# Gated cross-attention and a routed feed-forward: experts chosen in three batches, scatters begun inside attention, gathers issued pair by pair

## The chip, the cores and the metric

The kernel runs on one core of a Trainium2 chip. The metric is the device time of one execution in microseconds. "Span" is the time from the first to the last instruction of a profiled execution.

## The reference

```python
x = x + tanh(g_xattn) * attention(layernorm(x), ctx, ctx)       # x: 8 x 256 x 256, ctx: 8 x 77 x 256, 16 heads
n = layernorm(x)                                                # the kernel's x2
logits = n @ gate_w.T                                           # 8 experts
top_w, sel = top_k(softmax(logits), 2); top_w /= sum(top_w)
y = sum over the 2 chosen e of  w_e * (gelu(n @ W1[e] + b1[e]) @ W2[e] + b2[e])    # 256 -> 1024 -> 256
x = x + tanh(g_ffn) * (y + gelu(n @ sW1 + sb1) @ sW2 + sb2)     # + the shared expert, for every row
```

Everything is float32.

## The kernel before

The 2048 rows are `NT` = 16 tiles of 128. The kernel has two stages.

**Attention**, a software pipeline of steps `t` = 0 to 19. A step of PE holds the scores of tile t+1, the transposes and the weighted values of tile t, the projection of t-1, the transposes of the second layer norm's rows (`turn_x2`) of t-3 and the router's logits of t-4 (`route_logits`). DVE subtracts the maxima, normalises (L1242), adds the residual (`residual`, which waits on `x2_ready` of the tile ahead) and keeps the logits. ACT exponentiates and copies PSUM. POOL makes `x2row` (L461, `normal_two(t - 2)`), the layer-normed row tile; SP copies it into `x2` (`keep_x2`). POOL also loads the shared expert's weights in quarters and splits them into a high and a low part (`split_quarter_1`, `split_quarter_2`), in steps 5 to 12. Step 15 ends with `up(0)`, the first matmuls of the next stage.

**Expert stage**, `TILES` = 55 tiles of 128 rows: first `NA` = 9 "early" tiles through the shared expert, then `NR` = 39 "routed" tiles, grouped by expert, each expert's group padded to whole tiles, then `NB` = 7 "late" tiles through the shared expert. `R0` = 9 is the first routed tile and `R1` = 48 the first late one. For tile i PE runs `turn_hidden(i-1)` (L729, 8 transposes), `up(i)` (L741 to L743, 12 matmuls in two halves), `turn_rows(i+1)` (L722), `down(i-1)` (L754, L755, 16 matmuls). ACT copies the transposed hidden rows (L1111) and runs Gelu (L1117). DVE forms their low parts (L1271), adds b1 (L1277), forms the rows' low part (`rows_lo`, L1265) and makes the result (`ysum` L1387, `yrow` L1394, and for tiles of the shared expert L1400). SP loads each tile's rows two tiles ahead (`load_rows`), ACT stores a routed result to `routed_y` in HBM.

**Routing** stands between. After the last logits DVE picks the two experts of all 16 tiles (L1368 to L1383; `then` makes each operation wait for the one before). PE counts places with 17 small matmuls (`places`, in tile 1). `slots` (DVE, tile 1) turns counts into a destination row for each of the 4096 pairs of row and expert. `tables` and `tile_phases` (tiles 2 and 3) say which expert each tile has. POOL then issues 32 indirect DMAs (L619, the scatters: tile by tile, one for each of the two choices, 128 rows of 1 KB), which copy `x2` into `routed_x` in HBM. SP waits for all of them (`scattered`) before the first routed load. `routed_x` is zeroed by SP beforehand, in 6 parts after the `keep_x2` of steps of late attention (L363), since the padding rows must hold numbers.

After the last routed result is stored, POOL issues 32 indirect gathers (L655), and DVE adds them to the output in the late tiles (`combine`, L1416, two operations for each of the 16 tiles; `COMBINED` says in which late tile). `g_in[j]` counts the four gathers of output tiles 2j and 2j+1.

POOL also streams the experts' weights during the routed tiles (`phase`). Its queue is in order. Before the scatters it holds two quarters of `load_quarter_2` (L485, L486), four `split_quarter_1` (L491), four `split_quarter_2` (L497) and two loads of 1 MB.

## Time and profile before

| | us |
|---|---|
| median of three runs | 647.6 |
| lowest and highest of them | 638.16, 649.21 |
| the profiled execution | 643.06 |
| its span | 641.5 |
| PE busy | 551.5 (86%) |
| DVE, POOL, ACT busy | 357.8, 292.1, 242.0 |
| PE's mean granted clock | 0.91 of full |

Busy shares are means over stages that have different limits. The page's line of 40 slices shows where an engine is idle, the timeline shows which instruction ends an idle stretch, and the bracket behind a row gives how long its engine had been idle and what released it. "remote" in a bracket is a semaphore whose raising the trace can't place at that time.

### The profile page before, as it was taken

Reading aid. Unit: us, or ns where it says so; the run is one execution under the profiler, and the core shown is the slowest. Engines: PE = TensorE matmul, PEld = TensorE weight load, DVE = VectorE, ACT = ScalarE, POOL = GpSimd, SP = SyncE. Lnnn points to the kernel's source line nnn. Section 1 sums busy time; section 2 is a strip of 40 time slices with the busy share of each in tenths; the row PEclk is TensorE's granted clock in tenths of the full one; section 3 lists DMA queues with packets and bytes.
Section 4 is the critical chain, followed back from the end, with each engine's and each line's share of the span. In section 5 each row is a group of like instructions: output and inputs, shape, how many; then the busy total and the mean of one; then the engine's idle time right before and its main releaser. Section 6 shows DMA issues by size and latency. Waiting matters only on the chain.

```text
span 641.5 us, 12348 instructions
## 1 busy us (share of the span) xinstructions
PE 551.5 (86%) x3243; PEld 478.4 (75%) x3244; DVE 357.8 (56%) x735; ACT 242.0 (38%) x534; POOL 292.1 (46%) x267
## 2 busy tenths in 40 slices
PE   4799899998976841999999999999999999951496
PEld 3699899998965620888888888888888888840385
DVE  4346776655639510757556565565655655520398
ACT  3123576665641200333433334333333343310132
POOL 6226478885437774004354444444545430077300
PEclk9957799989886955899999999999999999995699
DMA  4752556567846332006556678486666640143211
GB/s 131 198 167 79 157 145 172 171 188 229 255 159 203 106 107 74 16 26 216 148 200 179 206 207 237 122 245 214 185 203 180 204 114 33 41 114 105 84 50 65
DMA packets 62216, 95.21 MB, mean 148 GB/s; under 512 B 6653, under 2 KB 47853, under 8 KB 62197
## 3 DMA queue, kind: packets, MB, share of 16 engines
q0 software_dynamic: 24800, 57.82, 30.7%
q1 hardware_dynamic: 28885, 29.77, 14.5%
q10 hardware_dynamic: 8512, 7.40, 3.8%
q8 instruction: 9, 0.15, 0.1%
q14 instruction: 10, 0.08, 0.0%
HBM read 68.15 MB, written 20.71 MB: 139 GB/s over the span
## 4 chain that ended last, share of the span: by engine, by line
PE 69%; DVE 9%; issue 8%; another core or an unknown queue 7%; ACT 3%; DMA 3%; ACTq 1%; POOL 0%; DVEq 0%; SPq 0%; POOLq 0%
PE ps L754 15%; PE ps L755 7%; PE ps L741 7%; PE ps L742 7%; PE ps L743 7%; PE ps L729 7%; PE ps L812 3%; PE ps L768 3%; PE ps L707 3%; PE ps L798 2%; PE ps L780 2%; PE ps L722 2%; DVE rt L1375 1%; DMA front<-in_ctx 1%
## 5 line engine op out<-in xcount | busy, mean ns | idle before, releaser
L754 PE MATMUL ps<-w2hl,hTh 128*128 (+1 forms) x440 | 164.6, 411 | 14.0 <-DVE hTl L1271 12.7
L1117 ACT ACTIVATE hid<-hid 128x512 f32<-128x512 f32 x110 | 69.2, 632 | 161.3 <-DVE hid L1277 150.3
L755 PE MATMUL ps<-w2hl,hTl 128*128 (+1 forms) x440 | 124.9, 284 | 0.0
L1111 ACT ACTIVATE hTh<-ps 128x512 fp32r<-128x512 f32 x110 | 60.1, 597 | 132.4 <-PE ps L729 87.6
L754 PEld LDWEIGHTS ps<-w2hl,hTh 128*128 128x128 f32 x440 | 84.2, 191 | 34.2 <-issue 16.9
L1277 DVE TENSOR_TENSOR hid<-ps,b1bc 128x512 f32<-128x512 f32 x110 | 75.3, 690 | 53.9 <-PE ps L743 22.4
L741 PE MATMUL ps<-w1l,xT 128*128 (+1 forms) x220 | 94.4, 429 | 11.1 <-issue 6.6
L742 PE MATMUL ps<-w1h,xT 128*128 (+1 forms) x220 | 89.1, 405 | 3.9 <-issue 3.9
L743 PE MATMUL ps<-w1h,xT 128*128 (+1 forms) x220 | 89.0, 404 | 3.0 <-issue 3.0
L755 PEld LDWEIGHTS ps<-w2hl,hTl 128*128 128x128 f32 x440 | 84.5, 192 | 0.0
L729 PE MATMUL ps<-ident,hid 128*128 128x128 f32 x440 | 60.2, 281 | 24.8 <-ACT hid L1117 18.9
L1271 DVE TENSOR_TENSOR hTl<-ps,hTh 128x512 fp32r<-128x512 f32 x110 | 71.0, 685 | 6.0 <-issue 6.0
L729 PEld LDWEIGHTS ps<-ident,hid 128*128 128x128 f32 x440 | 51.9, 145 | 29.0 <-ACT hid L1117 20.2
L1387 DVE TENSOR_TENSOR ysum<-ps,b2bc 128x256 f32<-128x256 f32 x55 | 23.3, 424 | 78.6 <-PE ps L755 45.0
L514 POOL TENSOR_TENSOR w2hl<-stage,w2hl 128x2048 f32 (+1 forms) x8 | 36.9, 4613 | 54.9 <-DMA w2hl<-in_L_ffn_W 49.8
L741 PEld LDWEIGHTS ps<-w1l,xT 128*128 128x128 f32 x220 | 42.9, 195 | 20.9 <-issue 8.7
L506 POOL TENSOR_TENSOR w1l<-stage,w1h 128x2048 f32 (+1 forms) x8 | 36.9, 4616 | 41.9 <-DMA w1h<-in_L_ffn_W 35.8
L743 PEld LDWEIGHTS ps<-w1h,xT 128*128 128x128 f32 x220 | 42.6, 194 | 13.5 <-issue 3.0
L742 PEld LDWEIGHTS ps<-w1h,xT 128*128 128x128 f32 x220 | 43.1, 196 | 11.1 <-issue 3.4
L1265 DVE TENSOR_TENSOR xT<-ps,xT 128x256 fp32r<-128x256 f32 x55 | 23.3, 424 | 50.0 <-ACT xT L1021 44.8
L655 POOL DMA_INDIRECT gath<-routed_y,slot x32 | 30.5, 952 | 44.2 <-DMA routed_y<-yrow 34.8
L812 PEld LDWEIGHTS ps<-spread_v,probT 128*128 128x128 f32 (+1 forms) x320 | 41.4, 199 | 1.2
(178 smaller groups left out, 846.2 us busy)
## 6 DMA issues: line engine op xcount, KB each, us to landing
stage<-in_L_ffn_W POOLq DMA_DIRECT2D x14, 1024.0 KB, 6.1
w1h<-in_L_ffn_W POOLq DMA_DIRECT2D x7, 1024.0 KB, 5.9
w2hl<-in_L_ffn_W POOLq DMA_DIRECT2D x7, 1024.0 KB, 8.4
qstack<-moved_q SPq DMA_DIRECT2D x48, 128.0 KB, 2.4
xrow<-routed_x SPq DMA_DIRECT2D x39, 128.0 KB
routed_y<-yrow ACTq DMA_DIRECT2D x39, 128.0 KB, 2.3
routed_x<-zeros SPq DMA_DIRECT2D x6, 768.0 KB, 5.8
moved_q<-hid SPq DMA_DIRECT2D x16, 256.0 KB, 3.6
```

The costliest lines, as they stand in the source:

```text
L506: pool.tensor_tensor(lo, stage1[:], hi.bitcast(F32), ALU.subtract).then_inc(S["split_w1"], 1)
L729: last = nc.tensor.transpose(p_hT[:, n, c, :], hid[:, n, c * P:(c + 1) * P], ident[:])
L741: mm(p_h[:, n, :], xTh[:, c, :], part(w1l, c), start=c == 0, stop=False)
L742: mm(p_h[:, n, :], xTh[:, c, :], part(w1h, c), start=False, stop=False)
L743: last = mm(p_h[:, n, :], xTl[:, c, :], part(w1h, c), start=False, stop=c == C - 1)
L754: mm(p_y, hTh[:, c, :], part(2 * D), start=c == 0, stop=False)
L755: last = mm(p_y[:, 0:D], hTl[:, c, :], part(D), start=False, stop=c == FC - 1)
L812: last = mm(p_o[:, h0:h1, :], probT[0:n, j, :], spread_v[0:n, at:at + h1 - h0, bass.ds(t // TB, 1), :].rearrange("k n o d -> k (n o) d"), ...
L1111: act.activation(hTh[:, n * (FC // 2):(n + 1) * (FC // 2), :], p_hT[:, n, :, :], ACT.Copy).then_inc(S["hT_hi"], 1)
L1117: act.activation(hid[:, n, :], hid[:, n, :], ACT.Gelu).then_inc(S["h_act"], 1)
L1271: tt(hTl[:, part, :], p_hT[:, n, :, :], hTh[:, part, :].bitcast(F32), ALU.subtract).then_inc(S["hT_lo"], 1)
L1277: tt(hid[:, n, :], p_h[:, n, :], b1bc[:, bass.ds(s, 1), n * (F // 2):(n + 1) * (F // 2)].rearrange("p o f -> p (o f)"), ALU.add).then_inc( ...
```

## The change

The experts are chosen in three batches of tiles, 0 to 7, 8 to 11 and 12 to 15. `choose(0)` runs at the end of DVE's attention step 11 and `choose(1)` at the end of step 15, each followed one step later by PE's `places(n)` and DVE's `slots(n)`; PE waits for `slots_set` at the start of the step after that. `choose(2)` stands where the one choice stood. `run` carries the counts from batch to batch.

A destination row no longer depends on all counts: `routed_x` has room for 17 tiles per expert (`CAP`), and each pair goes to expert * `CAP` plus its place. Only 8 tiles of padding are zeroed (`pad_row`), after `counts`. SP reads the row at which a routed tile begins from `src_row` with a `value_load`. The gathers use a second table, `y_slot`, since `routed_y` stays packed.

POOL issues twelve scatters of batch 0 by threes in its steps 13 to 16, with one quarter of `load_quarter_2` and one `split_quarter_1` each; then the other four, `load_w1` and `ready_1`, the 8 of batch 1 and the 8 of batch 2; then the four `split_quarter_2` and `load_w2`.

`NA` becomes 5, so `NB` becomes 11: 5 early, 39 routed, 11 late tiles, `R0` = 5, `R1` = 44. In the gathers POOL waits, before the four of a pair of output tiles, for the landing of the four before. `COMBINED` has eleven entries with at most two tiles each. Some tiles of SBUF are ordered anew, and the counts' PSUM lies in banks 5 and 7.

```diff
-    NA = NT // 2 + 1
+    NA = 5
...
+    CAP = (NT + 1) * P
+    BATCHES = ((0, 8), (8, 12), (12, NT))
+    CHOSEN_AFTER = (11, 15)
...
                 if kind == "routed":
-                    src = rows_v[bass.ds(i - R0, 1)].rearrange("o p d -> (o p) d")
+                    at = sp.value_load(src_row[0:1, bass.ds(i, 1)], min_val=0, max_val=E * CAP - P)
+                    src = rows[bass.ds(at, P), :]
...
-                part = rows_v[n * SHARE:min((n + 1) * SHARE, NR)]
-                sp.dma_start(part.rearrange("t p d -> p t d"), zeros[:].unsqueeze(1).to_broadcast(
-                    [P, part.shape[0], D])).then_inc(S["rows_zeroed"], 16)
-            in_pairs(sp, 2, R0, lambda i, parity: load_rows(i, parity, "early"))
+            load_rows(2, 0, "early")
+            load_rows(3, 1, "early")
+            sp.wait_ge(S["zero_set"], 1)
+            sp.wait_ge(S["pads_set"], 1)
+            for e in range(E):
+                at = sp.value_load(pad_row[0:1, e:e + 1], min_val=0, max_val=E * CAP - P)
+                sp.dma_start(rows[bass.ds(at, P), :], zeros[:]).then_inc(S["rows_zeroed"], 16)
+            in_pairs(sp, 4, R0, lambda i, parity: load_rows(i, parity, "early"))
+            sp.wait_ge(S["src_set"], 1)
+            sp.wait_ge(S["rows_zeroed"], 16 * E)
             sp.wait_ge(S["scattered"], 16 * TOP * NT)
...
-                if 13 <= t < 15:
+                if t == 12:
+                    pool.wait_ge(S["kd_ready"], 2 * B)
+                    pool.iota(tile_i[:], pattern=[[1, TILES], [0, PH - 1]], base=0, channel_multiplier=0
+                              ).then_inc(S["tiles_set"], 1)
+                if 13 <= t < 17:
                     load_quarter_2(1, first_w2, t - 13)
+                    split_quarter_1(1, t - 13)
+                    for n in range(3):
+                        scatter(0, 3 * (t - 13) + n)
+
+            def scatter(batch, n):
+                t, k = BATCHES[batch][0] + n // TOP, n % TOP
+                pool.wait_ge(S["slots_set"], batch + 1)
+                pool.wait_ge(S["x2_out"], 16 * (t + 1))
+                pool.indirect_dma_start(
+                    out=rows, out_offset=bass.IndirectOffsetOnAxis(ap=slot[:, k, t:t + 1], axis=0),
+                    in_=x2[:, t, :], in_offset=None).then_inc(S["scattered"], 16)
 
             for t in range(NT + 2):
                 step(t)
-            load_quarter_2(1, first_w2, 2)
-            load_quarter_2(1, first_w2, 3)
-            for q in range(4):
-                split_quarter_1(1, q)
+            for n in range(12, 16):
+                scatter(0, n)
             pool.wait_ge(S["split_w1"], 8)
             load_w1(2, expert_w1(1))
             ready_1(1)
+            for batch in (1, 2):
+                for n in range(TOP * (BATCHES[batch][1] - BATCHES[batch][0])):
+                    scatter(batch, n)
             for q in range(4):
                 split_quarter_2(1, q)
             pool.wait_ge(S["split_w2"], 8)
             load_w2(2, expert_w2(1))
             ready_2(1)
...
-            pool.wait_ge(S["slots_set"], 1)
-            pool.wait_ge(S["rows_zeroed"], 16 * NB)
-            pool.wait_ge(S["x2_out"], 16 * NT)
-            for t in range(NT):
-                for k in range(TOP):
-                    pool.indirect_dma_start(
-                        out=rows, out_offset=bass.IndirectOffsetOnAxis(ap=slot[:, k, t:t + 1], axis=0),
-                        in_=x2[:, t, :], in_offset=None).then_inc(S["scattered"], 16)
...
+            pool.wait_ge(S["y_slots_set"], 1)
             for t in range(NT):
+                if t % 2 == 0 and t:
+                    pool.wait_ge(g_in[t // 2 - 1], 16 * 2 * TOP)
                 for k in range(TOP):
                     pool.indirect_dma_start(
                         out=gath[:, t, k, :], out_offset=None, in_=routed_y,
-                        in_offset=bass.IndirectOffsetOnAxis(ap=slot[:, k, t:t + 1], axis=0)
+                        in_offset=bass.IndirectOffsetOnAxis(ap=y_slot[:, k, t:t + 1], axis=0)
                     ).then_inc(g_in[t // 2], 16)
...
+            def places(n):
+                t0, t1 = BATCHES[n]
+                wide, p_place = t1 - t0, p_places[n]
+                pe.wait_ge(S["chosen_set"], n + 1)
+                if n == 0:
+                    pe.wait_ge(S["q_sb"], NT)
+                if n == 1:
+                    pe.wait_ge(S["x2T_sb"], CHOSEN_AFTER[1] - 1)
+                mm(p_place[:, 0:wide + 1, :], before[:], chosen[:, t0 + n:t1 + n + 1, :], start=True, stop=False)
+                for u in range(wide):
+                    last = mm(p_place[:, u + 1:wide + 1, :], ones[:],
+                              chosen[:, t0 + n + u:t0 + n + u + 1, :].to_broadcast([P, wide - u, E]),
+                              start=False, stop=u == wide - 1)
+                last.then_inc(S["rank_ps"], 1)
...
+                if known and t - 2 in CHOSEN_AFTER:
+                    pe.wait_ge(S["slots_set"], CHOSEN_AFTER.index(t - 2) + 1)
...
+                if known and t - 1 in CHOSEN_AFTER:
+                    places(CHOSEN_AFTER.index(t - 1))
...
+            def choose(n):
+                t0, t1 = BATCHES[n]
+                some = [P, t1 - t0, E]
+                bc = lambda ap: ap.unsqueeze(2).to_broadcast(some)
+                far = iota_far[:].unsqueeze(1).to_broadcast(some)
+                if n == 0:
+                    dve.wait_ge(S["kd_ready"], 2 * B)
+                    dve.wait_ge(S["far_set"], 1)
+                    dve.memset(chosen[:], 0.0)
+                    dve.memset(run[:], 0.0)
+                dve.wait_ge(S["l_sb"], t1)
+                for k in range(TOP):
+                    lg = (logits, lg2)[k][:, t0:t1, :]
+                    then(dve.tensor_reduce(top[:, k, t0:t1], lg, AX_X, ALU.max))
+                    then(tt(rt[:, t0:t1, :], lg, bc(top[:, k, t0:t1]), ALU.is_equal))
+                    then(tt(rt[:, t0:t1, :], rt[:, t0:t1, :], far, ALU.mult))
+                    then(dve.tensor_reduce(pick[:, k, t0:t1], rt[:, t0:t1, :], AX_X, ALU.min))
+                    then(tt(hot[:, k, t0:t1, :], far, bc(pick[:, k, t0:t1]), ALU.is_equal))
+                    if k == 0:
+                        then(stt(lg2[:, t0:t1, :], hot[:, 0, t0:t1, :], -1e30, logits[:, t0:t1, :], ALU.mult, ALU.add))
+                tt(chosen[:, t0 + n:t1 + n, :], hot[:, 0, t0:t1, :], hot[:, 1, t0:t1, :], ALU.add
+                   ).then_inc(S["chosen_set"], 1)
+
+            def slots(n):
+                t0, t1 = BATCHES[n]
+                wide, p_place = t1 - t0, p_places[n]
+                dve.wait_ge(S["rank_ps"], n + 1)
+                then(tt(place[:, t0:t1, :], p_place[:, 0:wide, :], run[:].unsqueeze(1).to_broadcast([P, wide, E]), ALU.add))
+                then(tt(run[:], run[:], p_place[:, wide, :], ALU.add))
+                then(tt(onplace[:, :, t0:t1, :], hot[:, :, t0:t1, :],
+                        place[:, t0:t1, :].unsqueeze(1).to_broadcast([P, TOP, wide, E]), ALU.mult))
+                then(dve.tensor_reduce(posf[:, :, t0:t1], onplace[:, :, t0:t1, :], AX_X, ALU.add))
+                then(stt(slot_f[:, :, t0:t1], pick[:, :, t0:t1], float(CAP), posf[:, :, t0:t1], ALU.mult, ALU.add))
+                ts(slot[:, :, t0:t1], slot_f[:, :, t0:t1], FAR * CAP, None, ALU.add).then_inc(S["slots_set"], 1)
...
+                if isinstance(t, int) and t - 1 in CHOSEN_AFTER:
+                    slots(CHOSEN_AFTER.index(t - 1))
+                if isinstance(t, int) and t in CHOSEN_AFTER:
+                    choose(CHOSEN_AFTER.index(t))
...
+            choose(2)
+            rows_lo(1)
...
-            COMBINED = ((), (0, 1), (2, 3, 4), (5, 6, 7), (8, 9, 10), (11, 12), (13, 14, 15))
+            COMBINED = ((), (), (0, 1), (2, 3), (4, 5), (6, 7), (8, 9), (), (10, 11), (12, 13), (14, 15))
...
+            def counts():
+                slots(2)
...
+                then(stt(pad_f[:], iota_far[0:1, :], float(CAP), run[0:1, :], ALU.mult, ALU.add))
+                ts(pad_row[:], pad_f[:], FAR * CAP, None, ALU.add).then_inc(S["pads_set"], 1)
...
+            def sources():
+                then(dve.memset(step_up[:], 0.0))
+                then(ts(step_up[0:1, 1:E], etiles[0:1, 0:E - 1], -float(P), float(CAP), ALU.mult, ALU.add))
+                then(ts(limit[:], etiles[0:1, E - 1:E], float(P), float((E - 1) * CAP - P), ALU.mult, ALU.add))
+                then(tt(ups[:], started[0:1, :, 0:E], step_up[:].unsqueeze(1).to_broadcast([1, TILES, E]), ALU.mult))
+                then(dve.tensor_reduce(src_f[:, 0, :], ups[:], AX_X, ALU.add))
+                then(stt(src_f[:, 1, :], tile_f[0:1, :, 0], float(P), src_f[:, 0, :], ALU.mult, ALU.add))
+                then(ts(src_f[:, 0, :], src_f[:, 1, :], -float(R0 * P), None, ALU.add))
+                tt(src_row[:], src_f[:, 0, :], limit[:].to_broadcast([1, TILES]), ALU.min).then_inc(S["src_set"], 1)
...
+            def y_slots():
+                then(tt(onplace[:], hot[:], ebase[:].unsqueeze(1).unsqueeze(1).to_broadcast([P, TOP, NT, E]), ALU.mult))
+                then(dve.tensor_reduce(slot_f[:], onplace[:], AX_X, ALU.add))
+                stt(y_slot[:], slot_f[:], float(P), posf[:], ALU.mult, ALU.add).then_inc(S["y_slots_set"], 1)
...
+            def late_tables():
+                shares()
+                y_slots()
+
+            tile(1, "early", 0, 0, between=counts)
             tile(2, "early", 0, 0, between=tables)
-            tile(3, "early", 0, 0, between=tile_phases)
-            tile(4, "early", 0, 0, between=shares)
-            dve.wait_ge(S["tables_set"], 2)
+            tile(3, "early", 0, 0, between=sources)
+            tile(4, "early", 0, 0, between=late_tables)
```

## Rows read from the trace of the kernel before

**Rows 1.** The page's 40 slices of 16 us, PE's busy tenths

```profile
PE   4799899998976841999999999999999999951496
```

**Rows 2.** Table of stretches: stretch, its us, busy us of each engine, PE clock, DMA share, GB/s

```profile
300.00:500.00 200.00, 200.00 (x1137) 171.93 (x1135) 117.08 (x210) 78.49 (x151) 87.89 (x51) 1.00 0.65 196
...
560.00:610.00 50.00, 20.95 (x87) 15.30 (x85) 11.70 (x23) 6.24 (x13) 30.40 (x32) 0.68 0.34 97
```

**Rows 3.** Timeline of DVE, `ysum`: start us, us, engine, line, operation, idle before

```profile
217.56 0.42 DVE L1387 TENSOR_TENSOR ysum<-ps,b2bc 128x256 f32<-128x256 f32 x1 [2.42 <-remote]
...
255.28 0.42 DVE L1387 TENSOR_TENSOR ysum<-ps,b2bc 128x256 f32<-128x256 f32 x1 [20.31 <-remote]
...
563.31 0.42 DVE L1387 TENSOR_TENSOR ysum<-ps,b2bc 128x256 f32<-128x256 f32 x1 [0.95 <-issue]
...
605.60 0.42 DVE L1387 TENSOR_TENSOR ysum<-ps,b2bc 128x256 f32<-128x256 f32 x1 [9.80 <-remote]
...
612.78 0.42 DVE L1387 TENSOR_TENSOR ysum<-ps,b2bc 128x256 f32<-128x256 f32 x1 [0.31 <-PE ps L755]
...
620.13 0.42 DVE L1387 TENSOR_TENSOR ysum<-ps,b2bc 128x256 f32<-128x256 f32 x1
...
626.92 0.42 DVE L1387 TENSOR_TENSOR ysum<-ps,b2bc 128x256 f32<-128x256 f32 x1
```

**Rows 4.** Timeline of POOL: first and last of 32 scatters and of 32 gathers

```profile
209.52 1.09 POOL L619 DMA_INDIRECT routed_x<-x,slot  x1 [4.67 <-DVE slot L1453]
...
249.39 0.97 POOL L619 DMA_INDIRECT routed_x<-x,slot  x1 [0.30 <-issue]
...
559.94 1.02 POOL L655 DMA_INDIRECT gath<-routed_y,slot  x1 [34.80 <-DMA routed_y<-yrow]
...
598.90 0.95 POOL L655 DMA_INDIRECT gath<-routed_y,slot  x1 [0.30 <-issue]
```

**Rows 5.** Timelines of PE, ACT and DVE: PE's signals and who takes them

```profile
215.65 1.03 PE L729 MATMUL ps<-ident,hid 128*128 128x128 f32 x8
...
219.08 0.40 PE L743 MATMUL ps<-w1h,xT 128*128 128x512 f32 x1
...
219.68 0.60 ACT L1111 ACTIVATE hTh<-ps 128x512 fp32r<-128x512 f32 x1 [5.25 <-remote]
...
232.48 0.69 DVE L1277 TENSOR_TENSOR hid<-ps,b1bc 128x512 f32<-128x512 f32 x1 [6.35 <-remote]
...
563.11 1.03 PE L729 MATMUL ps<-ident,hid 128*128 128x128 f32 x8
...
568.68 0.60 ACT L1111 ACTIVATE hTh<-ps 128x512 fp32r<-128x512 f32 x1 [2.30 <-remote]
```

**Rows 6.** Table of stretches, behind the last scatter

```profile
251.50:252.00 0.50, 0.00 (x0) 0.00 (x0) 0.00 (x0) 0.00 (x0) 0.00 (x0) 0.50 0.00 0
```

**Rows 7.** Timeline of POOL: a split, and `x2row` in late attention steps

```profile
100.19 1.29 POOL L491 TENSOR_TENSOR w1l<-stage,w1h 128x512 fp32r<-128x512 f32 x1
...
170.44 0.77 POOL L485 DMA_DIRECT2D stage<-in_L_ffn_W  x1
...
175.07 1.21 POOL L461 TENSOR_SCALAR x2row<-xres,mv,nw 128x256 f32<-128x256 f32 x1 [3.14 <-ACT nw L1044]
...
187.65 1.22 POOL L461 TENSOR_SCALAR x2row<-xres,mv,nw 128x256 f32<-128x256 f32 x1 [5.13 <-ACT nw L1044]
```

**Rows 8.** Timeline of DVE: two operations of the choice of experts

```profile
197.97 5.02 DVE L1375 TENSOR_TENSOR rt<-lg,top 128x128 f32<-128x128 f32 x1
...
203.03 0.29 DVE L1376 TENSOR_TENSOR rt<-rt,iota_far 128x128 f32<-128x128 f32 x1
```

**Rows 9.** Timeline of DVE: one normalisation per attention step

```profile
149.80 0.42 DVE L1242 TENSOR_TENSOR o_n<-ps,rsum 128x256 f32<-128x256 f32 x1
...
157.71 0.42 DVE L1242 TENSOR_TENSOR o_n<-ps,rsum 128x256 f32<-128x256 f32 x1
...
167.60 0.42 DVE L1242 TENSOR_TENSOR o_n<-ps,rsum 128x256 f32<-128x256 f32 x1
```

More of the change, by code:

```diff
@@ L923, in _ @@
                 step(t, t % 2)
-            def places():
-                pe.wait_ge(S["chosen_set"], 1)
-                mm(p_place, before[:], chosen[:], start=True, stop=False)
-                for u in range(NT):
-                    last = mm(p_place[:, u + 1:NT + 1, :], ones[:],
-                              chosen[:, u:u + 1, :].to_broadcast([P, NT - u, E]), start=False, stop=u == NT - 1)
-                last.then_inc(S["rank_ps"], 1)
             def phase_at(i):
@@ L954, in _ @@
             turn_rows(1, 1)
-            tile(1, 1, (0, 0), (0, 0), places)
+            tile(1, 1, (0, 0), (0, 0), lambda: places(2))
             in_pairs(pe, 2, R0, lambda i, parity: tile(i, parity, (0, 0), (0, 0)))
@@ L1436, in tile @@
                 result(i - 1, phase_at(i - 1) if last is None else last, kind)
-            def slots():
-                dve.wait_ge(S["rank_ps"], 1)
-                then(ts(cnt_i[:, 0, :], p_place[:, NT, :], float(P - 1), None, ALU.add))
+            def counts():
+                slots(2)
+                then(ts(cnt_i[:, 0, :], run[:], float(P - 1), None, ALU.add))
                 then(ts(cnt_i[:, 1, :], cnt_i[:, 0, :], 7, None, ALU.logical_shift_right))
```

74 lines of the change are left out of this document (28 added, 46 removed).

## The prediction

> **What bounds the kernel now.** I read the page first: in [rows 1] TensorE is full in nearly all 40 slices of 16 us, but two stretches are almost empty, slices 15 to 16 (225 to 257 us) and slices 36 to 38 (560 to 610 us). The table of stretches [rows 2] shows them against a full one: from 300 to 500 us PE is busy for all 200 us at full clock, from 560 to 610 us for 20.95 of 50.
>
> Next the list of `ysum`, one per tile of the expert stage. From tile 2 (255.28) to tile 48 (563.31) there are 46 tiles in 308.03 us [rows 3]: 6.70 us a tile, with PE never idle. So PE sets the pace, and the change leaves PE's work on the 55 tiles alone. What it can move are the two gaps: tile 1 to tile 2 took 37.7 us, 31.0 more than 6.7 (the first gap); tile 48 to tile 49 took 42.3, 35.6 more (the second gap) [rows 3]. The time after is that of now less what of these 66.6 us comes back, plus what the new work costs.
>
> Then what runs beside each gap. POOL issues its 32 scatters from 209.52 to 250.36 and its 32 gathers from 559.94 to 599.85 without a pause, one each 1.27 us [rows 4]. Nobody waits for their data in either gap. What comes late is PE's word to the others [rows 5]. The transposes of one tile begin at 215.65, and ACT, which starts 0.6 us into them in a quiet tile, starts at 219.68; the last matmul of `up` begins at 219.08, and DVE's add of its second half is at 232.48, 13 us late. In the gather series the second half of the transposes begun at 563.11 reaches ACT at 568.68, 4.5 us late. So PE's signals are prompt for some 3.4 us, late by 2 to 5 us at an age of 4 to 7 us, and after about 15 us everybody stands. It ends at 255.28, 4.9 us after the last scatter, and at 605.60, 5.7 us after the last gather, although the DMA engines moved nothing after 251.5 [rows 6]. I take the cause as "a long unbroken series of indirect DMAs holds up PE's signals". I don't know the path on which they meet.
>
> **The change, part by part, against the profiled execution** (643.1 us, of which the span is 641.5; the three runs have their median at 647.6 and their lowest at 638.2, so the one stands between them and I take the sum as the forecast of the median).
>
> *A, attention: +5.* Sixteen scatters of batch 0 become ready at step 12; twelve are issued by threes in POOL's steps 13 to 16, with the four `split_quarter_1` (1.29 us each [rows 7]). POOL's step 14 then holds 1.2 of `x2row`, 1.5 of two loads (0.77 each), 1.3 of split and 3.8 of scatters, 7.8 us, and the steps there are 6.3 us apart (175.07 to 187.65 in two) [rows 7]. POOL's slack is used up in step 14, `x2row` is then late by 2, 3.5 and 5 us, and the last one (187.65) carries the last logits: +5 (0 if the steps stretch anyway, 8 at most). DVE's `residual` queues behind `x2_ready`, and PE's next scores behind DVE; I count that in the same 5. `choose` is 13 operations; uncontended, they lie 0.32 us apart [rows 8], 4.2 us for each early batch on DVE. DVE is half idle in these steps, so 1 us is charged for two. `slots(0)` isn't hidden: PE has just run `places(0)` (9 small matmuls, at 0.13 us like the transposes of [rows 5] or twice that: 1 to 2 us) and stops at the next step for six DVE operations, 1.9 us; the second batch lies in steps that wait for the `x2row` chain. Together +4 with the other batch's matmuls. To the credit: SP's zeroing of 5 MB (39 tiles of 128 KB) beside these steps is gone; eight writes of 128 KB remain, behind the early loads. The step that ends at 167.60 took 9.9 us, its forerunner 7.9 [rows 9], and nothing shows that it was the zeroing: I credit 3 (0 to 5). The last batch's `choose(2)` handles 4 tiles and not 16. In the trace one of these two-input operations took 5.03 us beside POOL's four splits, where 0.30 is normal [rows 8]. POOL scatters there after the change. I credit 2, less than half of that stall, since `rows_lo(1)`, for which PE waits, stands ahead of it in DVE's queue. Sum 5+1+4-3-2 = +5, bounds -3 and +15.
>
> The row of 5.03 us is weighed against the Trainium skill, "SBUF — State Buffer", on the shared port pair: an operation of VectorE with both inputs in SBUF and a GpSimd operation that reads SBUF block each other, the later for the whole of the earlier. By that rule the stalls move with the splits: `choose(1)` in step 15 runs beside a split of 1.29 us and would pay up to that much. By the row's whole price (5.03) A would be 9, by the rule at most 6.3.
>
> *B, the first gap: 31 becomes 16.* After step 17 POOL issues 4 and 8 scatters in one series (12 x 1.27 = 15.3 us), stops for `slots_set` of the last batch, and issues 8 more (10.2 us). The first series loses what it outlasts the prompt time: 15.3, plus 2 to 5 us to clear, less the 7 to 9 for which work goes on: 10. DVE's `slots(2)` itself waits for PE's `rank_ps` through this, so the 8 can't join the 12. They lose 10.2 plus 3 less 7: 6. Bounds: 5 (both short series are borne as the first 8 us of the long one were) and 31. Behind the waiting POOL stand `split_quarter_2`, `load_w2` and `ready_2(1)`; they end near 235 us, and `down` of tile 5 wants them near 255: covered by 20 us, and without that cover their 6 us would show. The routed rows wait for the scatters' landing near 230, behind tiles 2 to 4 (3 x 6.7 us): covered.
>
> *C, longer DVE chains in early tiles 1 to 4: +2.* `counts` has 13 operations for 9, `sources` 8 more, `tables` takes over three. DVE is busy 117.08 of 200 us [rows 2], so it has 2.8 us to spare in a tile of 6.7; each chain goes over that by about 0.5 (0 and 6 as bounds). SP's extra `value_load` before each routed load costs nothing: the load is two tiles ahead (13 us); without that cover it costs its own latency, once.
>
> *D, the second gap: 35.6 and 1.1 of slow clock behind it become 6.* Four gathers take 3 x 1.25 us to the last issue, which lands after some 2.1 us (the last scatter was issued at 249.39 [rows 4], and nothing moved after 251.5 [rows 6]). With 0.7 for the wait's own latency a pair has 6.6 us, the eight 53 us. They start 3.4 us before the first late tile's `ysum`, like now, and eleven late tiles give 74 us: pair n is wanted about 13 + 6.7n us after that `ysum` and a step later from pair 5 on, so the combining waits for nothing; at a period of 10 us it would wait some 15 at the end. What remains is lateness inside a burst of 4.7 us: signals late by 2 to 4.5 us, where PE's order (`turn_hidden`, then `up` from 216.7 to 219.5, then `down`) bears about 2, which is these 2.8 less ACT's 0.6 [rows 5]. That is 0 to 2 a burst; I take 0.75, so 6. Clearing in the pause is my assumption: 32 in a row needed 4.9 us to clear, 0.15 each, so 4 need 0.6, and the pause is 1.9.
>
> *E, -1.* Combining three outputs stretched a late tile to 7.35 us, two leave it at 6.79 [rows 3], and the last tile now combines two for three.
>
> Sum: 5 - 15 + 2 - 30.7 - 1 = -39.7, and 643.1 - 39.7 gives **603 us**, 0.93 of the median. Its own range is 590 to 620.
>
> **Rivals.**
> *Standstill doesn't clear in a pause (slower).* If the 4.9 us behind a series are fixed, whatever its length, then a pause of 1.9 us between pairs clears nothing, and neither do the 4 us between the threes in attention. For it: both long series show nearly the same tail (4.9 and 5.7). Against it: the lateness grows through the series, as a backlog does. Price: the paced gathers stand for 53 + 5.5 - 8 = 50 us, 14 over now; four attention steps lose 3.8 + 4.9 - 3.4 = 5.3 each, 21; the two series of B lose 13 and 12. 643.1 + 5 + 21 - 6 + 14 + 2 - 1 = 678. It decides as soon as clearing takes more than 1.9 us behind four.
> *A paced burst costs its lateness in full.* Each of the eight costs the 4.5 us of the second half's signal: 36 instead of 6, 633 us. The change then would not do what it says: the gap is only spread out. The rows at 568.68 speak for it, PE's 2 us of slack against it.
> *Short series are free.* B falls to 5 and D to 0: 603 - 11 - 6 = 586. For it are the 3.4 prompt us and 6 us of nearly normal work in the gather series.
>
> The Trainium skill, "Runtime: NRT & Kernel Launch", on instruction fetch, offers another reading of the first rival: instructions stream in pages through a DMA queue, and fetch suffers where execution leaves the window. That would hit the unrolled attention steps and late tiles, of which the change adds; its time would be that rival's. No row here shows such a fetch. Since PE itself ran on (219.08) while DVE had its signal 13 us late [rows 5], I give that reading no chance of its own.
>
> **Chances.** Forecast 0.48, short series free 0.13, lateness in full 0.20, no clearing 0.19. A run under about 635 counts as faster, over 660 as slower (2% is about what this kernel's spread lets one tell). The third case lies across 635; a quarter of it is faster. Faster 0.48 + 0.13 + 0.05 = 0.66, same 0.15, slower 0.19. The range from 584 to 648 leaves out the last case and a little below.
>
> **What the profile after would show.** D right: gathers by fours over 50 to 56 us, PE busy in nine tenths there, late tiles at 6.7 to 8 us. B right: tile 2's `ysum` near 245 and two stretches of idle PE with a run of tiles between. A right: last logits near 196. The rival of no clearing: PE at a few tenths through all eleven late tiles, and attention steps 13 to 16 over 10 us. Lateness in full: late tiles at 10 to 11 us. The forecast would be wrong above all if pauses of 2 us do nothing, or if twelve scatters inside attention hold its chain more than they occupy POOL.

## The result, and the profile after

| | before | after |
|---|---|---|
| median of the runs | 648.4 us (638.16 to 653.22) | 600.03 us (596.85 to 600.65) |
| profiled execution, its span | 643.1 us, 641.5 us | 599.54 us, 597.9 us |
| last logits (end of attention) | 191.28 | 204.61 |
| `ysum` of tile 2 | 255.28 | 247.40 |
| `ysum` of tile 44 (the first late one after) | 536.69 | 527.36 |
| `ysum` of tile 54 (the last) | 637.94 | 594.33 |

The ratio is 0.932, with an interval of 0.919 to 0.945. The ratio leaves out executions in the slower state that a kernel is sometimes in, at a lower granted clock, so it isn't the quotient of the medians: they differ by 48.4 us, the executions that the ratio compares by 43.5. The spans of the two profiled executions differ by 43.6 us. From this table: attention ends 13.3 us later; from there to tile 2 it is 42.8 us where it was 64.0 (-21.2); tiles 2 to 44 take 279.96 where they took 281.41 (-1.4); tiles 44 to 54 take 66.97 where they took 101.25 (-34.3).

The page's slices of the kernel after, 15 us each; `PEclk` is the granted clock in tenths:

```profile
PE   4799899999788573999999999999999999999996
PEclk9765999999879585999999999999999999999999
```

Against [rows 1] the second hole has gone: from slice 17 to the end PE is full. The first has shrunk to slices 14 to 16, and slices 11 and 12, in attention, have thinned to 7 and 8.

Table of stretches of the kernel after, columns as in [rows 2]:

```profile
151.80:164.10 12.30, 8.25 (x60) 7.37 (x59) 10.00 (x26) 5.55 (x17) 4.54 (x6) 0.86 0.52 157
164.10:175.70 11.60, 9.59 (x56) 9.39 (x57) 6.26 (x16) 4.91 (x14) 7.07 (x7) 0.71 0.40 126
204.00:230.00 26.00, 15.72 (x70) 12.30 (x70) 8.15 (x33) 4.99 (x10) 20.50 (x22) 0.70 0.48 165
...
524.00:578.00 54.00, 53.46 (x301) 45.26 (x300) 40.73 (x81) 19.43 (x39) 30.52 (x32) 1.00 0.40 118
```

The last row answers to 560 to 610 in [rows 2]: the same 32 gathers occupy POOL for the same 30.5 us, but PE is busy for 53.46 of 54 us, and at full clock (1.00, that is 2.4 GHz) where it had 0.68. The third row is the first hole: PE works 15.72 of 26 us.

Timeline of DVE after, `ysum`, to be held against [rows 3]:

```profile
231.05 0.42 DVE L1447 TENSOR_TENSOR ysum<-ps,b2bc 128x256 f32<-128x256 f32 x1 [13.87 <-remote]
...
247.40 0.40 DVE L1447 TENSOR_TENSOR ysum<-ps,b2bc 128x256 f32<-128x256 f32 x1
...
527.36 0.42 DVE L1447 TENSOR_TENSOR ysum<-ps,b2bc 128x256 f32<-128x256 f32 x1 [0.92 <-issue]
534.61 0.42 DVE L1447 TENSOR_TENSOR ysum<-ps,b2bc 128x256 f32<-128x256 f32 x1 [0.22 <-issue]
542.61 0.42 DVE L1447 TENSOR_TENSOR ysum<-ps,b2bc 128x256 f32<-128x256 f32 x1 [0.59 <-issue]
...
594.33 0.42 DVE L1447 TENSOR_TENSOR ysum<-ps,b2bc 128x256 f32<-128x256 f32 x1 [0.81 <-PE ps L780]
```

There is now one standstill, 13.87 us long, ahead of tile 0. The ten steps from 527.36 to 594.33 are 6.70 us in the mean (from 5.25 to 8.14), against 6.67 in the steady part.

Timeline of POOL after, with [rows 4] beside it: first and last of the one long series of scatters, then the first burst of gathers and the start of the second:

```profile
202.39 1.08 POOL L625 DMA_INDIRECT routed_x<-x,slot  x1 [0.18 <-issue]
...
227.55 0.97 POOL L625 DMA_INDIRECT routed_x<-x,slot  x1 [0.30 <-issue]
...
524.02 1.03 POOL L680 DMA_INDIRECT gath<-routed_y,y_slot  x1 [33.36 <-DMA routed_y<-yrow]
...
527.87 0.95 POOL L680 DMA_INDIRECT gath<-routed_y,y_slot  x1 [0.30 <-issue]
530.86 0.94 POOL L680 DMA_INDIRECT gath<-routed_y,y_slot  x1 [2.05 <-DMA gath<-routed_y,y_slot]
```

Timelines of PE, ACT and DVE after, the signals that [rows 5] show for before:

```profile
216.49 1.04 PE L754 MATMUL ps<-ident,hid 128*128 128x128 f32 x8
...
215.20 0.17 DVE L1361 TENSOR_SCALAR slot<-slot_f 128x8 int32<-128x8 f32 x1
...
231.12 1.09 ACT L1147 ACTIVATE hTh<-ps 128x512 fp32r<-128x512 f32 x2 [15.92 <-remote]
...
529.88 1.09 ACT L1147 ACTIVATE hTh<-ps 128x512 fp32r<-128x512 f32 x2 [3.89 <-remote]
```

The transposes of 216.49 reach ACT at 231.12, 2.6 us after the last scatter of the long series has ended (228.52). In the paced gathers the late transposes reach ACT at 529.88, 1.06 us after the fourth gather has ended (528.82), while the pause is still running. The third line is for the prediction's step B: the last batch's slots are there at 215.4, while POOL, in the 8 scatters of the second batch, doesn't ask for them before 218.6.

### The profile page after: what moved, and what is told of

It is laid out like the page before. It is cut to its first block, busy times and chain, and to the rows that moved or that the text cites. A ratio compares the mean times of both kernels' runs of the same rounds, so it can differ in the third digit from the quotient of the medians.

```text
span 597.9 us, 12619 instructions
## 1 busy us (share of the span) xinstructions
PE 545.3 (91%) x3245; PEld 476.1 (80%) x3246; DVE 362.2 (61%) x787; ACT 241.8 (40%) x534; POOL 292.9 (49%) x267
## 4 chain that ended last, share of the span: by engine, by line
PE 70%; POOL 9%; issue 9%; DMA 3%; another core or an unknown queue 3%; DVE 3%; ACT 1%; ACTq 1%; SPq 1%; POOLq 0%; DVEq 0%
PE ps L779 17%; PE ps L780 8%; PE ps L766 8%; PE ps L767 8%; PE ps L768 8%; PE ps L754 8%; PE ps L732 3%; POOL x2row L480 2%; PE ps L747 2%; PE ps L793 2%; POOL xn L463 1%; POOL routed_x L625 1%; POOL w1l L510 1%; DMA moved_q<-hid 1%
## 5 line engine op out<-in xcount | busy, mean ns | idle before, releaser
L779 PE MATMUL ps<-w2hl,hTh 128*128 (+1 forms) x440 | 162.4, 409 | 15.8 <-DVE hTl L1307 15.6
L780 PE MATMUL ps<-w2hl,hTl 128*128 (+1 forms) x440 | 123.5, 281 | 0.0
L766 PE MATMUL ps<-w1l,xT 128*128 (+1 forms) x220 | 92.8, 422 | 0.6 <-issue 0.6
L767 PE MATMUL ps<-w1h,xT 128*128 (+1 forms) x220 | 87.9, 400 | 0.0
L768 PE MATMUL ps<-w1h,xT 128*128 (+1 forms) x220 | 87.7, 399 | 0.0
L754 PE MATMUL ps<-ident,hid 128*128 128x128 f32 x440 | 58.2, 276 | 0.0
L680 POOL DMA_INDIRECT gath<-routed_y,y_slot x32 | 30.5, 954 | 55.7 <-DMA routed_y<-yrow 33.4
L768 PEld LDWEIGHTS ps<-w1h,xT 128*128 128x128 f32 x220 | 41.9, 191 | 10.3
L767 PEld LDWEIGHTS ps<-w1h,xT 128*128 128x128 f32 x220 | 42.2, 192 | 7.5
```

Of the source, the lines that this page charges most:

```text
L754: last = nc.tensor.transpose(p_hT[:, n, c, :], hid[:, n, c * P:(c + 1) * P], ident[:])
L766: mm(p_h[:, n, :], xTh[:, c, :], part(w1l, c), start=c == 0, stop=False)
L767: mm(p_h[:, n, :], xTh[:, c, :], part(w1h, c), start=False, stop=False)
L768: last = mm(p_h[:, n, :], xTl[:, c, :], part(w1h, c), start=False, stop=c == C - 1)
L779: mm(p_y, hTh[:, c, :], part(2 * D), start=c == 0, stop=False)
L780: last = mm(p_y[:, 0:D], hTl[:, c, :], part(D), start=False, stop=c == FC - 1)
```

## The experiments

Each was timed beside the kernel before on the same chip; a ratio is to that. All runs keep the whole computation unless their expectation says otherwise.

**Which part makes the gain.** First the kernel after without its wait between pairs of gathers:

```diff
             for t in range(NT):
-                if t % 2 == 0 and t:
-                    pool.wait_ge(g_in[t // 2 - 1], 16 * 2 * TOP)
                 for k in range(TOP):
```

> The changed kernel, but its 32 gathers are issued in one series again (the wait for the pair in front is gone). Theory (a long unbroken series holds up PE's signals, a pause of 2 us clears them): the second gap comes back in the late tiles with the 35 us that it had before the change, so about 635 us, with one late tile some 40 us behind the one in front. Rival (the gain at the end comes from the eleven late tiles instead of seven, which cover the gathers, and the pacing does nothing): about 600, late tiles at 6.7 us.

Measured: 633.48 us, ratio 0.982 (0.974 to 0.990). The wait alone is worth 33 us, of the 44 to 48 that the whole change brings. DVE's `ysum` of the kernel without it:

```profile
527.09 0.42 DVE L1445 TENSOR_TENSOR ysum<-ps,b2bc 128x256 f32<-128x256 f32 x1 [0.91 <-issue]
569.37 0.42 DVE L1445 TENSOR_TENSOR ysum<-ps,b2bc 128x256 f32<-128x256 f32 x1 [9.99 <-remote]
```

The gap is 42.28 us, that of before to a hundredth (42.29 in [rows 3]).

Whose signals come late can be read inside the long series of the kernel before, ACT and PE at an age of 17 us, then PE at 32 to 34 us:

```profile
226.16 0.63 ACT L1117 ACTIVATE hid<-hid 128x512 f32<-128x512 f32 x1 [4.40 <-DVE hid L1277]
226.84 1.11 PE L729 MATMUL ps<-ident,hid 128*128 128x128 f32 x4 [2.64 <-ACT hid L1117]
...
241.93 0.39 PE L742 MATMUL ps<-w1h,xT 128*128 128x512 f32 x1 [2.18 <-issue]
244.03 0.59 PE L743 MATMUL ps<-w1h,xT 128*128 128x512 f32 x1 [1.71 <-issue]
```

ACT starts 0.04 us after DVE's add has ended (226.12), and PE 0.05 us after ACT (226.79). So DVE's and ACT's signals are prompt in there, and only PE's are late. Later PE itself slows: where its matmuls lie 0.43 us apart at 238, they come one per 2.1 to 2.8 us from 239.14 on (one per 1.4 to 2.8 us in the run without the wait, from 563.65 on, just behind its last gather), with nothing in the trace that they wait for. So PE runs on at first, but not through the whole series.

The other way round, the kernel before with that wait and nothing else:

```diff
             for t in range(NT):
+                if t % 2 == 0 and t:
+                    pool.wait_ge(g_in[t // 2 - 1], 16 * 2 * TOP)
                 for k in range(TOP):
```

> The kernel before, with the pacing of the gathers alone; 9 early and 7 late tiles, one choice. Theory: PE's gap goes, but 8 pairs at 6.75 us end 54 us after their start, at 614, and seven late tiles give only 47 us: combining waits for data, the last result comes near 618, in all about 624 us. Rival (pacing does nothing, or more late tiles are what counts): 640 or more.

Measured: 625.9 us, ratio 0.970 (0.961 to 0.978), as the theory had it. It is worth less here (some 20 us) than in the kernel after: the late tiles at 579.58, 590.28 and 598.36 lie 10.7 and 8.1 us apart where 6.7 is the pace, and the gathers end at 622.4, only 4 us before the last `ysum` (626.55). Combining waits for data, because this kernel has fewer tiles of work behind the start of its gathers.

Then the kernel before with both series by fours, each four waiting until those in front have landed:

```diff
             for t in range(NT):
+                if t % 2 == 0 and t:
+                    pool.wait_ge(S["scattered"], 16 * TOP * t)
                 for k in range(TOP):
```

> The kernel before, gathers paced as in the change, and its 32 scatters paced too, each four after the landing of the four in front; nothing else. Theory: the scatters take 54 us instead of 41, from 209.5 to 264, PE works on through the early tiles (tile 8 at about 265 instead of 295) and then waits some 5 to 10 us for the first routed rows; with the late tiles of the run before this one about 605 us. Rival (choosing in batches and scattering inside attention are what closed the first gap): first gap as before, about 624.

Measured: 608.28 us, ratio 0.941 (0.932 to 0.950). Two waits in the old kernel thus bring some six sevenths of what the whole change brings (0.059 of 0.068 in the ratio, and the two intervals overlap). What they lack is seen at one place: tiles 0 to 6 follow each other at 6.7 us (`ysum` 217.86 to 257.84), and the next is at 281.60, since the 32 paced scatters end at 269 and the routed rows can be loaded only then (PE waits 14.94 us for them; the profiled execution is the longest of the four, with a span of 615.3 us). That is what the change's scatters inside attention are good for.

**How long may a series be.** The gathers of the kernel after in bursts of eight:

```diff
-                if t % 2 == 0 and t:
+                if t % 4 == 0 and t:
```

> The changed kernel, but the gathers wait for the landing of those in front after every eight, not every four. Theory as a backlog (each indirect DMA adds a little to what must clear, and PE's signals are late once a series is some 4 us old): each of the four series of 10 us holds PE's signals from about 4 us on until 1.5 us after its end, of which PE bears 2 us; 3 to 6 us a series, so 612 to 624 us. Rival (a fixed threshold near 15 us of series, as where everybody stood in the kernel before): 600, late tiles at 6.7 us.

Measured: 619.94 us, ratio 0.964 (0.959 to 0.969). Its `ysum` of the first late tiles:

```profile
529.61 0.42 DVE L1447 TENSOR_TENSOR ysum<-ps,b2bc 128x256 f32<-128x256 f32 x1 [0.91 <-issue]
544.01 0.42 DVE L1447 TENSOR_TENSOR ysum<-ps,b2bc 128x256 f32<-128x256 f32 x1 [3.41 <-remote]
558.79 0.42 DVE L1447 TENSOR_TENSOR ysum<-ps,b2bc 128x256 f32<-128x256 f32 x1 [4.23 <-remote]
572.86 0.42 DVE L1447 TENSOR_TENSOR ysum<-ps,b2bc 128x256 f32<-128x256 f32 x1 [5.76 <-remote]
```

Three tiles of 14.1 to 14.8 us for 6.7. The next two come at 6.1, and the ten late tiles take 87.2 us where the kernel after takes 67.0: four bursts of eight cost 20 us more than eight of four, 5 each, which is what the time is slower by. The rival on record, a threshold near 15 us, falls. The price of one gather isn't fixed either: against the 65.1 us that the ten late tiles take where nothing disturbs them (two experiments further on), 32 gathers cost 1.9 us in bursts of four, 22 in bursts of eight and 37 in one series. That fits the theory's backlog, of which PE's slack takes the first part.

**Is it the landing or the pause.** The wait on the data replaced by something that only takes POOL's time, a memset of 1.8 us ordered on itself:

```diff
                 if t % 2 == 0 and t:
-                    pool.wait_ge(g_in[t // 2 - 1], 16 * 2 * TOP)
+                    pool.wait_ge(S["consts"], 13 + t // 2)
+                    pool.memset(stage1[:], 0.0).then_inc(S["consts"], 1)
```

> The changed kernel; between the pairs' gathers POOL does not wait for landing but writes 2048 zeros per partition to a staging tile that nobody reads any more (1.8 us as in the zeroing of a tile of that size at the start). The gap between the last of four issues and the next is then the same 2 us. Theory (it is the pause in POOL's generating that counts): 600 us. Rival (it counts that no indirect DMA is under way): the four overlap the pause in part, 600 too, but with late tiles of 8 us and more if landings matter, up to 620.

Measured: 602.26 us, ratio 0.936 (0.932 to 0.941), late tiles at 6.68 us (530.92 to 597.72). Two us in which POOL issues no indirect DMA are enough, and no wait is needed. Whether it is POOL's pause or the landing of the four isn't separated: the memset leaves 1.98 us between the bursts and the wait on landing 2.05, so the four have landed, or nearly, either way.

**Is it indirect DMAs, or any DMA from POOL.** The 32 gathers replaced by 32 plain transfers of the same size, with no wait between them:

```diff
-                if t % 2 == 0 and t:
-                    pool.wait_ge(g_in[t // 2 - 1], 16 * 2 * TOP)
                 for k in range(TOP):
-                    pool.indirect_dma_start(
...
+                    pool.dma_start(gath[:, t, k, :], y_v[TOP * t + k]).then_inc(g_in[t // 2], 16)
```

> The changed kernel with 32 plain DMAs in place of the 32 gathers, issued by POOL in one series without a pause, each 128 rows of 1 KB from consecutive rows of routed_y (so the outputs take the wrong expert rows; the work of all engines is the same). Theory (the indirect form is what holds up PE's signals): the series takes about 25 us and PE doesn't notice it, about 597 us. Rival (any unbroken series of small DMAs from POOL does): a gap of 20 us and more, 620 or more.

Measured: 600.49 us, ratio 0.934 (0.927 to 0.941). POOL and ACT of this kernel:

```profile
527.88 16.95 POOL L678 DMA_DIRECT2D gath<-routed_y  x32 [35.03 <-DMA routed_y<-yrow]
...
531.63 1.09 ACT L1142 ACTIVATE hTh<-ps 128x512 fp32r<-128x512 f32 x2 [1.81 <-PE ps L749]
538.31 1.09 ACT L1142 ACTIVATE hTh<-ps 128x512 fp32r<-128x512 f32 x2 [1.81 <-PE ps L749]
544.98 1.08 ACT L1142 ACTIVATE hTh<-ps 128x512 fp32r<-128x512 f32 x2 [1.81 <-PE ps L749]
```

The plain series lasts 17 us without a pause, and ACT's work on `hTh` stays at its pitch of 6.67 us; in an indirect series everything stands at that age. So it isn't POOL's issuing of DMAs as such, nor the bytes or their number of rows. What is left is the indirect form, with one thing not separated from it: the plain transfers also read consecutive rows. The ten late tiles take 65.08 us here (531.20 to 596.28), the last ones being shorter, and that is their undisturbed time. The Trainium skill, "DMA: Bandwidth & Descriptors", section "SWDGE vs HWDGE vs iDMA", has GpSimd build the descriptors of every DMA that it issues, direct or indirect, and write them into rings in SBUF; by this run that shared path alone isn't where the signals are held. On which path they meet stays open.

**The first gap.** The kernel after with its last 20 scatters by fours as well:

```diff
                 t, k = BATCHES[batch][0] + n // TOP, n % TOP
+                done = TOP * BATCHES[batch][0] + n
+                if done >= 12 and done % 4 == 0:
+                    pool.wait_ge(S["scattered"], 16 * done)
                 pool.wait_ge(S["slots_set"], batch + 1)
```

> The changed kernel, and its last 20 scatters, which it issues in one series from 202 to 228.5 us, go by fours, each after the landing of those in front. Theory: the series grows from 26 to about 34 us, to 237, but tiles 0 to 2 come at 6.7 to 9 us and not 14 us late: tile 2 near 233 instead of 247; the first routed rows then come 2 to 5 us late. In all 587 to 592 us. Rival (a series of 20 is short enough, and the gap at 217 to 231 us comes from the late choice of the last batch): 600, or 605 through the later landing.

Measured: 593.28 us, ratio 0.925 (0.913 to 0.936); the runs are 591.17, 592.89, 593.67 and 601.56, those of the kernel after lie from 596.85 to 600.65. DVE and POOL of this kernel:

```profile
232.62 0.42 DVE L1450 TENSOR_TENSOR ysum<-ps,b2bc 128x256 f32<-128x256 f32 x1 [0.60 <-PE ps L783]
...
233.54 5.75 DVE L1463 SCALAR_TENSOR_TENSOR xres<-yrow,tgate,xres 128x256 f32<-128x256 f32 x1
...
244.66 0.42 DVE L1450 TENSOR_TENSOR ysum<-ps,b2bc 128x256 f32<-128x256 f32 x1 [0.67 <-PE ps L783]
...
234.04 4.96 POOL L516 TENSOR_TENSOR w2hl<-stage,w2hl 128x512 fp32r<-128x512 f32 x4
```

No standstill is left: the last logits are at 204.73 and tile 2's `ysum` at 232.62, 27.9 us for the 42.8 after. Of these 14.9 us one tile gives back 5.3 (232.62 to 244.66 is 12.0 for 6.7), because POOL's four `split_quarter_2`, which now begin just there, hold one operation of DVE for 5.75 us where it takes 0.48 elsewhere. In the same stretch PE waits 0.88 us for tile 4's rows and 2.45 for the first routed rows (at 238.70). The Trainium skill, "SBUF — State Buffer", section "Who interferes with whom", says that a VectorE operation with two inputs in SBUF and a GpSimd operation that reads SBUF exclude each other for the whole of one instruction; the trace agrees with the exclusion, but one instruction of POOL takes 1.24 us here, and DVE was held through all four, although its record begins 0.5 us ahead of the first.

So the four splits were spread, one into each of four pauses:

```diff
                 scatter(0, n)
+            split_quarter_2(1, 0)
...
                 for n in range(TOP * (BATCHES[batch][1] - BATCHES[batch][0])):
+                    if n == 4:
+                        split_quarter_2(1, batch)
                     scatter(batch, n)
-            for q in range(4):
-                split_quarter_2(1, q)
+                if batch == 1:
+                    split_quarter_2(1, 3)
```

> The changed kernel with its last 20 scatters by fours as in the run that measured 593 us, and with the four weight splits that stood behind them put one each into the pauses between the fours. In that run DVE's update of xres took 5.75 us beside the four splits in a row (0.48 otherwise) and tile 3 came 12 us after tile 2. Theory: the splits hide in the pauses, that wait is at most 1.3 us, tile 3 follows 7 us after tile 2: about 588 us. Rival (tile 3 is late because of the routed rows' loading): 593.

Measured: 594.18 us, ratio 0.925 (0.920 to 0.930), the same as without. The theory fell. PE and SP of this kernel:

```profile
229.63 0.44 PE L753 MATMUL ps<-ident,xrow 128*128 128x128 f32 x2 [2.57 <-DMA xrow<-x]
239.43 0.69 PE L753 MATMUL ps<-ident,xrow 128*128 128x128 f32 x2 [2.87 <-DMA xrow<-routed_x]
...
217.43 10.12 SPq L382 DMA_DIRECT2D routed_x<-zeros  x8
227.59 0.52 SPq L332 DMA_DIRECT2D xrow<-x  x1
236.40 1.97 SPq L332 DMA_DIRECT2D xrow<-routed_x  x2
```

DVE's long operation at this place is gone, and PE waits longer for rows instead: 2.57 us (0.88 in the run before) for early tile 4, whose load stands behind eight writes of zeros in SP's queue, and 2.87 (2.45) for the first routed rows. The load was then put ahead of the writes:

```diff
             load_rows(3, 1, "early")
+            load_rows(4, 0, "early")
             sp.wait_ge(S["zero_set"], 1)
...
-            in_pairs(sp, 4, R0, lambda i, parity: load_rows(i, parity, "early"))
```

> The kernel after with its last 20 scatters by fours on landing, four split_quarter_2 put one each in the pauses, and SP's load of early tile 4 moved ahead of its eight writes of zeros. With the load behind the writes the tiles 2, 3 and 4 ended at 233.09, 244.04 and 252.31, and PE waited 2.57 us for tile 4's rows and 2.87 for the first routed rows. Theory: SP's queue of writes (they end at 227.5) holds the load of tile 4: then tile 3 follows tile 2 by about 8 us and the time is 590. Rival: the load waits for something else (its buffer, or PE's signal that the one before is transposed), or the routed rows' load, which waits for the scatters to land, takes the gain back: 594, as without the edit.

Measured: 593.46 us, ratio 0.917 (0.912 to 0.923): the rival's number. PE of this kernel:

```profile
240.59 0.69 PE L753 MATMUL ps<-ident,xrow 128*128 128x128 f32 x2 [5.96 <-DMA xrow<-routed_x]
```

The first wait is gone and the second has taken it over, 5.96 us for 2.57 and 2.87. The routed rows' load is issued at 236.14 here (236.40 without the edit), behind the last scatter at 232.5. The bound of this stage is the end of the paced scatters, which SP awaits before that load; the splits and the queue of SP only shared a wait that was there anyway. The best version is the kernel after with its last scatters paced, about 593.5 us with or without the two further edits.

**Attention.** The version with paced scatters, with none of them inside attention; all 32 follow step 17 by fours:

```diff
                     split_quarter_1(1, t - 13)
-                    for n in range(3):
-                        scatter(0, 3 * (t - 13) + n)
...
-                if done >= 12 and done % 4 == 0:
+                if done and done % 4 == 0:
...
-            for n in range(12, 16):
+            for n in range(16):
```

> The kernel after with its last 20 scatters by fours on landing, and its first 12, which stood by threes in attention steps 13 to 16, moved behind step 17 too: all 32 then go by fours, eight fours of some 6.7 us. Attention ended 140.9 us after tile 0's o_n in the kernel after and 132.2 before. Theory: POOL's 3.8 us of scatters a step make x2row late and carry the last logits, some 5 us of the 9; so the last logits come near 136 us behind tile 0's o_n. The 32 take 54 us, so the first tile with routed rows (tile 5) waits some 15 to 20 us: about 603. Rival: the choice of the first batch and PE's waits for its positions and places make up all of the excess; then the last logits stay at 141 us behind tile 0's o_n and the time is about 608.

Measured: 607.29 us, ratio 0.939 (0.934 to 0.945). Attention ended 142.5 us after tile 0's `o_n` (61.69 to 204.21), so the rival's numbers are nearer; how far its reason carries is read from the rows. PE of the kernel after in steps 12, 13 and the last ones:

```profile
157.39 0.44 PE L860 MATMUL ps<-ident,x2row 128*128 128x128 f32 x2 [3.38 <-DVE logits L1319]
...
166.11 1.02 PE L866 MATMUL ps<-gateT,bv_bc 128*128 128x8 f32 x4 [2.17 <-DVE slot L1361]
...
202.36 0.66 PE L860 MATMUL ps<-ident,x2row 128*128 128x128 f32 x2 [3.27 <-POOL x2row L480]
```

and PE and POOL of the one without scatters there, in the last steps:

```profile
198.14 1.02 PE L867 MATMUL ps<-gateT,bv_bc 128*128 128x8 f32 x4 [2.46 <-DVE slot L1362]
...
198.59 1.22 POOL L480 TENSOR_SCALAR x2row<-xres,mv,nw 128x256 f32<-128x256 f32 x1 [3.11 <-ACT nw L1081]
```

Without the scatters POOL waits for ACT (3.11 us) and no longer PE for POOL. From `o_n` of tile 13 (177.74) to the last logits it takes 26.5 us, against 28.9 in the kernel after (from 175.72) and in every other run with the scatters inside attention: the scatters make 2.4 us there. How much the second batch's choice and slots make can't be read off in the same way, since the old attention took 23.7, 29.9 and 26.6 us for this stretch in its three traces (before, and the two with waits added).

The first batch's share is clearer. The step from tile 11's to tile 12's `o_n`, behind `choose(0)`, took 7.91 us in each of the old attention's three traces and 12.3 to 14.9 in the nine of the new one: 14.35 here, where no scatter has been issued yet, and 12.34 in the kernel after. Whole executions of the same code differ by some 3 us in this, so a single pair of traces can't carry the sum over attention. Behind attention the theory's other half holds: one tile takes 24 us (`ysum` 237.19 to 261.17), in which PE waits 15.71 us for routed rows behind the 32 scatters, which end at 252.

## Why the prediction was right or wrong, point by point

**The number.** 603 predicted, 600.0 measured; but two of its terms missed in opposite directions, by +8 and by some -8, so that the total came this close is luck. What was right and is shown is the mechanism of its largest term, D.

**A, attention: +5 predicted, +13.3 measured, step mis-sized.** 4.6 us of it lie ahead of tile 0's `o_n` (59.10 before, 63.72 after), where the change altered nothing; kernels with the same code there had that row anywhere from 59.0 to 66.1, so this is scatter between executions. The change's own part is 8.7 us in this pair of traces; from tile 0's `o_n` to the last logits the old attention took 132.2 to 134.5 us in three traces and the new one, with its scatters inside, 140.9 to 145.0 in eight. The prediction's chain through a late `x2row` is there (3.27 us on PE above), but the scatters made 2.4 us through it where the sum had 5. The mis-sized term is the one for the choice and the slots, 1 + 4: the one step behind `choose(0)` alone grew by 4.4 us (7.91 to 12.34), and by up to 7.0 in other runs. PE waited 3.38 us until `logits` was copied behind `choose(0)`, and 2.17 us for `slots(0)`. The prediction took DVE's half-idle time as cover and charged one microsecond for two. But PE's next step hung on a copy of 0.16 us queued behind the 14 operations (the prediction counted 13), and then the queue counts, not DVE's average load. The credit of 3 us for SP's removed writes isn't shown: the step of 9.9 us in [rows 9] became 11.6, and in the two kernels that keep the writes and only add waits it took 5.88, with another step the long one (9.85 and 8.79 us). One operation of `choose(0)` took 2.04 us beside POOL's work (its like takes 0.24):

```profile
153.24 0.24 DVE L1345 TENSOR_TENSOR hot<-iota_far,pick 128x64 f32<-128x64 f32 x1
...
154.96 2.04 DVE L1345 TENSOR_TENSOR hot<-iota_far,pick 128x64 f32<-128x64 f32 x1
```

**B and C, last logits to tile 2: -13 predicted, -21.2 measured, and by another course.** "Stops for `slots_set` of the last batch" failed. The last batch's slots were ready at 215.4, ahead of the standstill and 3 us before POOL wanted them, so the two short series were one of 20 scatters, 26 us long. What was left of the standstill is 14.9 us (42.8 less the 27.9 of the version with paced scatters), where B and C together left 18. That these are close is luck in part: the step put 16 on two stretches that never were. The gain came out larger than 13 since by the same 27.9 us the stretch of before (64.0) held 36.1 us too much, and not 31. The other 5 lie mostly ahead of tile 0: from the last logits to its `ysum` it was 18.2 us (191.28 to 209.47), against 12.3 to 13.9 in the three versions with twelve scatters inside attention and the others paced. There the choice for all 16 tiles stood before, with the 5.02 us of [rows 8]; the sum had credited its going with 2. The kernel before with both series paced, which keeps that choice, still takes 17.95 us (199.91 to 217.86; 17.1 with the gathers alone paced), so this part doesn't come from the scatters' pacing; that it is the choice is argued from the rows.

**D and E, the late tiles: -31.7 predicted, -34.3 measured between tiles 44 and 54.** The mechanism is shown: the wait makes the gain, in either kernel, and a pause without a wait makes it as well. The size was off by the 0.75 us a burst: the ten late tiles took 66.97 us against the undisturbed 65.08, so eight bursts cost 1.9 us together and not 6. PE's 2 us of slack cover nearly all of a burst's lateness (ACT's first late transposes start 2.1 us late, at 529.88 for 527.16 + 0.6). The pause was 2.05 us where 1.9 was taken (the 0.7 us in it for the wait itself came from no row), a pair's period 6.7 to 6.8 (once 7.5) for 6.6. Of the 1.1 us that D books as slow clock, 0.65 are the stretched tile of E once more: at 612 to 620 us the granted clock was 1.00. A further 1.4 us come from tiles 2 to 44 at 6.67 us for 6.70, which wasn't predicted and which no run here explains.

**The rivals.** That the standstill doesn't clear in a pause is refuted by the row at 529.88. The time to clear grows with the length of the series: 1.06 us after 4, 2.6 after 20, 4.9 and 5.7 after 32 ([rows 3, 4]; 5.76 in the run without the wait). "Lateness in full" (633) is refuted by the late tiles. "Short series are free" was nearly right for the gathers (1.9 us for eight); for the scatters no short series came about until they were paced, and then the freed time was partly taken back by another wait. The reading by instruction fetch finds nothing in the unrolled late tiles, which run at 6.70 us; that it would hit unrolled code in the first place was the prediction's own step.

## What to carry to other kernels

Break a long series of indirect DMAs by pauses of about 2 us after every four, since here bursts of four cost 0.2 us each, bursts of eight some 5 and 32 in a row 36. Start early, because pacing stretches 32 of them from 41 us to between 51 and 53, and the data may then be the bound. When two engines' chains hold a step together, taking the load off one shows only the difference to the other. And an operation put in a half-idle engine's queue is not covered, if a short copy that the critical engine waits for stands behind it.

## What the runs showed of the hardware

- An unbroken series of indirect DMAs (one per 1.27 us, 128 rows of 1 KB each) holds back PE's signals to ACT and DVE, while DVE's and ACT's own stay prompt (0.05 us at an age of 17 us). PE goes on at first; from an age of 30 us among the scatters, and just behind 32 gathers, it issues one matmul per 1.4 to 2.8 us. Plain DMAs of the same size from the same engine, one per 0.53 us, don't hold the signals back, over 17 us.
- The effect depends on the length of the series: 0.2 us for each burst of 4 with pauses of 2 us, 5 us for each burst of 8, and ACT and DVE nearly at a stop for lack of PE's signals from an age of about 15 us.
- DVE was held 5.75 us by four operations of POOL of 1.24 us each, and got no turn between them.
- Tile 0's `o_n` moved between 59.0 and 66.1 us from one execution to another with the same instructions ahead of it, and the step behind `choose(0)` between 12.3 and 14.9 us over nine traces.
